# Mixed mLSTM and MLP block on one core: head stacks placed behind the first four MLP tiles, gate weights in one 128-column tile, decay exponents in half precision

## The chip, the cores and the metric

The kernel runs on one core of one Trainium2 chip. The metric is the device time of one launch in microseconds (us). A core has a matrix engine, TensorE (PE; its weight loads are shown apart as PEld), a vector engine (DVE), a scalar engine (ACT), GpSimd (POOL), and the DMA queues, here all issued by SyncE (SP). The engines run on their own and meet at semaphores.

## The reference, cut to what matters

The input is x of 8 sequences, 1024 tokens, 512 features, in float32. Everything reads one layer norm of x, and two branches are added to x:

```python
xn = _layernorm(x, axis=-1)
x = x + _L0_attn_ref(xn, Wq, Wk, Wv, Wog, Wig, big, Wfg, bfg, gamma, Wout) \
      + _L0_ffn_ref(xn, w_gate, w_up, w_down)
# attention: mLSTM, 8 heads, 32 query/key and 64 value features each
i_pre = soft_cap(x @ Wig.T + big)
f_pre = soft_cap(x @ Wfg.T + bfg)
f_log = log_sigmoid(f_t); m_new = maximum(f_log + m, i_t)
F = exp(f_log + m - m_new); I = exp(i_t - m_new)
C_new = F * C + (I * k_t) v_t;  n_new = F * n + I * k_t
h = einsum(q_t * scale, C_new) / (maximum(|q_t * scale . n_new|, exp(-m_new)) + EPS)
y = (sigmoid(x @ Wog.T) * headnorm(h) * gamma) @ Wout.T
# MLP, hidden size 2048
einsum(silu(gate) * up, w_down)
```

## The kernel before

The 8192 tokens are cut into 32 blocks of 256, and one hardware loop per engine runs 32 times over the blocks (`Fori(0, NB)`). The weights are loaded and split once, ahead of the loops. Each operand of a large product is kept as a high and a low half-precision part, and a product is three matmuls (`three`, L1006 to L1008: high by high, high by low, low by high). The recurrence is computed in chunks of 128 tokens.

What PE does in one block is written out by hand: the gate pre-activations (L1062 and L1064, eight matmuls), q and k (48 matmuls of 256 columns), v (24 matmuls of 512 columns), and then the 16 MLP tiles `ffn0` to `ffn15`, 24 matmuls of 256 columns each. The down projection of tile j, `down(j)`, six matmuls of 512 columns, stands behind tile j + 2. Pieces of the mLSTM stand behind given MLP tiles; a table of lists, `AFTER`, says which, and every engine walks through the same table. In it `stack3` is a piece for DVE alone, `stats` the layer norm statistics of the next block, `wT` and `wbc` the transpose and the spreading of the decay weights, `kT` the transpose of k, `es0` to `es3` the exponents and scores of two chunks and two groups of heads.

For tile j, ACT takes the tanh of the gate half (L640), DVE makes two products with the PSUM bank (L879, L882; the second one releases the bank), ACT writes the high part (L644), POOL the low part (L530), and `down(j)` waits for that. Three PSUM banks, `work0` to `work2`, go round in the order of the list `USES`.

The head stacks: `stack(h)` is six DVE copies (L828 and L829 in turn) that put the high and low parts of q and k of head h of a group above one another in `qq` and `kk`, for the score matmul L1134. Three stacks stand ahead of `ffn0` in DVE's program, behind the two operations that make the low parts of q (L866) and k (L868), and the fourth behind `ffn0`. The score matmul of `es0` waits for all 24 copies. In `wT` DVE writes `we_r` (L896, L898), which PE's L1111 (`wbc`) waits for.

The decay exponents: for each pair of tokens of a chunk and each head the exponent is one matmul of 512 columns, L1128, of `pair_l` and `pair_r` into `e_bank`. They hold the terms as a rounded high part and a rest in the 32-bit format F32R. DVE writes `pair_l`, `uhl` and `a_hi` (L855 to L862); POOL writes `pair_r` from `uhl` and a diagonal (`pair`, L520), once before `ffn0`, and once behind `es1`.

The gate weights lie in one tile of 104 columns per slice of 128 features: high parts in columns 0 to 39, low parts from column 64 (`G_LOW`). L1062 uses all 104 columns with the high part of x, L1064 only the first 40 with the low part. ACT copies the rows from 64 on (L606) and DVE adds them to the first 40 (L833), which frees the bank.

Of the kernel before, what the change touches and what calls it, by code (L numbers as in the profile page):

```python
# [16 lines left out]
ALU = mybir.AluOpType  # L17
ACT = mybir.ActivationFunctionType
AX = mybir.AxisListType
F32 = mybir.dt.float32  # L20
F32R = mybir.dt.float32r
F16 = mybir.dt.float16
# [4 lines left out]
P = 128  # L27
D = 512
KC = D // P
BATCH, SEQ = 8, 1024  # L30
BLOCK = 256
# [3 lines left out]
NH, DQ, DV = 8, 32, 64  # L35
# [7 lines left out]
GR = 40  # L43
G_LOW = 64
# [34 lines left out]


AFTER = {j: [] for j in range(NJ)}
AFTER[0] = ["stack3"]
AFTER[2] = ["stats"]
AFTER[3] = ["wT"]
AFTER[4] = ["wbc", "kT", "es0"]
AFTER[5] = ["o0", "mean_var"]
AFTER[6] = ["es1", "pv0", "xn0"]
# [69 lines left out]
def mlstm_mlp_kernel(nc, x, w_dram, gate_bias, gamma, out):  # L157
    ctx = ExitStack()
    with ctx:
        def sb(name, shape, dt):  # L160
            return ctx.enter_context(nc.sbuf_tensor(name, shape, dt))
# [6 lines left out]


        wt = {n: sb(f"parts_{n}", [P, 2, c], F16) for n, c in WCOLS.items() if n != "gates"}  # L170
        w_gates = sb("parts_gates", [P, KC, G_LOW + GR], F16)
        w_qk = wt["qk"][:, :, :].rearrange("p h (k f) -> p h k f", k=KC)
        w_v = wt["v"][:, :, :].rearrange("p h (k f) -> p h k f", k=KC)
        w_o = wt["o"][:, :, :].rearrange("p h (k f) -> p h k f", k=KC)
# [29 lines left out]
        xt = sb("xt", [P, KC, 2, BLOCK], F16)  # L204
        we_r = sb("we_r", [GR, BLOCK], F32R)

        pair_r = sb("pair_r", [P, NH, P], F32R)
        pair_l = sb("pair_l", [P, BLOCK], F32R)

# [6 lines left out]
        at, off = {}, 0  # L218
# [31 lines left out]
        tg, lf, ip, bc, mm, wr = (at[n] for n in ("tg", "lf", "ip", "bc", "mm", "wr"))  # L250
        uu, aa = bc, ip
        we = at["tg"]
        uhl = at["uhl"].bitcast(F32R)
        a_hi = at["lf"].bitcast(F32R)
        state = at["state"].rearrange("p (g n) -> p g n", g=NG)
        upd = at["upd"]
        num = at["num"].rearrange("p (h e) -> p h e", h=NH)
# [102 lines left out]
        def bank(name):  # L360
            return work[bank_no(name)]
# [54 lines left out]
        def _(pool):  # L416
            g = nc.gpsimd
# [3 lines left out]
            def link(ins):  # L421
                own_k[0] += 1
                ins.then_inc(pool_set, 1)
                pool.wait_ge(pool_set, own_k[0])
# [20 lines left out]
                                     base=-first, pattern=[[-HG, NG], [-1, HG], [0, DQ]], channel_multiplier=1))  # L445
            link(g.memset(we_r[:, :].bitcast(F32), 0.0))
            link(g.memset(w_gates[:, :, GR:G_LOW], 0.0))
            link(g.memset(diag[:, :], 0.0))
            for first in (0, 32):
                link(g.affine_select(out=diag[:, :], in_=diag[:, :], compare_op=ALU.not_equal, fill=1.0, base=-first,  # L450
                                     pattern=[[-1, NH]], channel_multiplier=1))
            link(g.memset(pair_r[:, :, :].bitcast(F32), 0.0))
            for first in (64, 96):
                link(g.affine_select(out=pair_r[:, :, :], in_=pair_r[:, :, :].bitcast(F32),
                                     compare_op=ALU.not_equal, fill=1.0, base=-first,
                                     pattern=[[-1, NH], [0, P]], channel_multiplier=1))
            link(g.memset(pair_l[:, :].bitcast(F32), 0.0))
            link(g.memset(pair_l[0:NH, :].bitcast(F32), -1.0))
            link(g.memset(pair_l[32:32 + NH, :].bitcast(F32), -1.0))
            link(g.memset(own_head[:, :], 0.0))  # L460
            for h in range(HG):
                link(g.memset(own_head[h * DQ:(h + 1) * DQ, h * VW:(h + 1) * VW], 1.0))
# [25 lines left out]

            for name in ("qq", "kk", "wr", "tg", "state"):
                link(g.memset(at[name], 0.0))  # L490
            link(g.memset(uhl.bitcast(F32), 0.0))
            for r, names in enumerate(ROUNDS):

                a, b = pieces_before(names[0]), pieces_before(names[-1], PIECES[names[-1]])
# [20 lines left out]
            with pool.Fori(0, NB) as i:  # L515
                own = Count(pool_own, 8)

                def pair(c):

                    g.tensor_tensor(pair_r[0:GR, :, :],  # L520
                                    uhl[0:GR, c * P:(c + 1) * P].bitcast(F32).unsqueeze(1).broadcast_to((GR, NH, P)),
                                    diag[0:GR, :].unsqueeze(2).broadcast_to((GR, NH, P)),
                                    ALU.mult).then_inc(pair_ready, 1)

                pool.wait_ge(parts_ready, i + 1)
                pair(0)
                for j in range(NJ):

                    pool.wait_ge(h_hi, i * NJ + j + 1)  # L529
                    g.tensor_tensor(hh[:, j % HB, 1, :], tt[:, j % 2, :], hh[:, j % HB, 0, :],  # L530
                                    ALU.subtract).then_inc(h_ready, 1)
                    for step in AFTER[j]:
                        if step.startswith("es"):

                            k = int(step[-1])
                            pool.wait_ge(exp_done, START + i * 4 + k + 1)
                            own.step(g.tensor_tensor(begun[0:1, 15:16], half_pow[0:1, 0:1], half_pow[0:1, 1:2],  # L537
                                                     ALU.add))
                            rows = pm[:, k % 2, :].rearrange("p (h t) -> p h t", h=HG)
                            g.affine_select(out=rows, in_=rows, compare_op=ALU.is_ge, fill=0.0, base=0,  # L540
                                            pattern=[[0, HG], [1, P]], channel_multiplier=-1).then_inc(masked, 1)
                        if step == "es1":

                            pool.wait_ge(e_full, i * 4 + 2)
                            pair(1)
                        if step.startswith("scale"):

                            pool.wait_ge(var_ready, i * NCH + int(step[-1]) + 1)
                            g.tensor_tensor(rd, var, half_pow[:, :], ALU.pow).then_inc(rd_ready, 1)  # L549
                        if step == "mean_var":  # L550

                            pool.wait_ge(stats_ready, NCH * (i + 2))
                            norm_factors(i, own)
                own.close()
# [130 lines left out]
        def _(dve):  # L685
            d = nc.vector

            k = [0]
# [131 lines left out]
            with dve.Fori(0, NB) as i:  # L820
                own = Count(dve_own, DVE_OWN)

                def stack(h):

                    rows = slice(h * DQ, (h + 1) * DQ)
                    for n, (q_part, k_part) in enumerate(((0, 0), (1, 0), (0, 1))):
                        to_ = slice((h + n) % HG * DQ, ((h + n) % HG + 1) * DQ)
                        d.tensor_copy(qq[to_, :, h, :], qp[rows, q_part, :, :]).then_inc(stacks_ready, 1)  # L828
                        d.tensor_copy(kk[to_, :, h, :], kp[rows, k_part, :, :]).then_inc(stacks_ready, 1)  # L829
# [17 lines left out]
                for c in range(NCH):  # L847
# [10 lines left out]
                own.settle(dve, i)  # L858
                own.step(d.tensor_scalar(m_carry, mm[0:NH, BLOCK - 1:BLOCK], keep[0:NH, bass.ds(i + 1, 1)], None,
                                         ALU.mult))  # L860
                own.step(d.tensor_tensor(uhl[32:32 + NH, :], uu[0:NH, :], uhl[0:NH, :].bitcast(F32), ALU.subtract))
                d.tensor_tensor(pair_l[96:96 + NH, :], aa[0:NH, :], a_hi[0:NH, :].bitcast(F32),  # L862
                                ALU.subtract).then_inc(parts_ready, 1)

                dve.wait_ge(qk_hi, 2 * (i + 1))
# [2 lines left out]
                own.step(d.scalar_tensor_tensor(out=kp[:, 1, :, :], in0=kf, scalar=unscale[:, NS + 2:NS + 3],  # L868
                                                in1=kp[:, 0, :, :], op0=ALU.mult, op1=ALU.subtract))
                own.settle(dve, i)  # L870
                stack(0)
                stack(1)
                stack(2)

                for j in range(NJ):

# [7 lines left out]
                                           op1=ALU.mult).then_inc(free_of(f"ffn{j}"), 1)  # L884
                    for step in AFTER[j]:
                        k_ = int(step[-1]) if step[-1].isdigit() else 0
                        if step == "stack3":
                            stack(3)
                        elif step == "stats":

                            dve.wait_ge(x_loaded, 16 * (i + 2))
# [32 lines left out]
                        elif step.startswith("pv"):  # L924

                            c, g = k_ // 2, k_ % 2
# [74 lines left out]
        def _(pe):  # L1001
            t = nc.tensor
# [32 lines left out]
            with pe.Fori(0, NB) as i:  # L1035
# [23 lines left out]
                pe.wait_ge(work_free[bank_no("xT1")], START + i * uses_of(bank_no("xT1")))  # L1059

                for k in range(KC):
                    t.matmul(bank("gates")[0:G_LOW + GR, 0:BLOCK], w_gates[:, k, :], xt[:, k, 0, :], start=(k == 0),  # L1062
                             stop=(k == KC - 1), skip_group_check=True)
                    mm_ = t.matmul(bank("gates")[0:GR, 0:BLOCK], w_gates[:, k, 0:GR], xt[:, k, 1, :], start=False,  # L1064
                                   stop=(k == KC - 1), skip_group_check=True)
                mm_.then_inc(work_full, 1)
                for name, f in (("q", 0), ("k", NH * DQ)):
                    wait_bank(pe, i, name)
                    for g in range(NG):
                        mm_ = by_feature(bank(name)[:, g * BLOCK:(g + 1) * BLOCK], w_qk, f + g * P, f + (g + 1) * P)  # L1070
# [5 lines left out]
                for j in range(NJ):  # L1076
# [5 lines left out]
                    for k in range(KC):  # L1082
                        if j in UNIT_IN:


                            c, g = UNIT_IN[j] // 2, UNIT_IN[j] % 2
                            mm_ = t.matmul(o_bank[:, k * VW:(k + 1) * VW], pm[:, UNIT_IN[j] % 2, k * P:(k + 1) * P],
                                           v[:, c, g * HG + k, :], start=False, stop=(k == HG - 1),
                                           skip_group_check=True)
# [7 lines left out]
                    for step in AFTER[j]:  # L1097
                        k = int(step[-1]) if step[-1].isdigit() else 0
# [8 lines left out]
                        elif step == "wbc":  # L1107

                            pe.wait_ge(we_split, i + 1)
                            for g in range(NG):  # L1110
                                mm_ = t.matmul(bank(step)[:, g * BLOCK:(g + 1) * BLOCK], spread[0:GR, g, :],  # L1111
                                               we_r[:, :], start=True, stop=True)
# [9 lines left out]
                        elif step.startswith("es"):  # L1122
                            c, g = k // 2, k % 2
# [5 lines left out]
                                     stop=True).then_inc(e_full, 1)  # L1129
# [9 lines left out]
                        elif step.startswith("pv"):  # L1139
                            c, g = k // 2, k % 2  # L1140
# [65 lines left out]
```

## Time and profile before

| | |
|---|---|
| time before, median of 3 runs | 3277.08 us (3275.98 to 3279.02) |
| the profiled execution: its time | 3273.61 us |
| the profiled execution: its span | 3271.9 us |
| mean granted TensorE clock | 0.992 of full speed |
| busy over the span: PE | 3101.0 us, 95% |
| PEld | 2229.5 us, 68% |
| DVE | 1876.5 us, 57% |
| ACT | 1116.8 us, 34% |
| POOL | 768.3 us, 23% |
| DMA | 51.08 MB, mean 16 GB/s |

The span goes from the first to the last instruction; the time of the execution lies 1.7 us above it. Matmuls are pipelined: the next one of a row starts before the record of the one before ends, so what a matmul costs is read from start to start. Line numbers are those of the kernel before.

### The profile page before, as it was taken

To read this page: it belongs to the slowest core of one execution; us is meant where nothing else is said; L and a number is where in the kernel's file an instruction comes from. 1 tells how busy PE (TensorE), PEld (TensorE's weight loads), DVE (VectorE), ACT (ScalarE), POOL (GpSimd) and SP (SyncE) were. 2 spreads that over 40 slices of the span, in tenths; PEclk is the share of its full clock that TensorE was granted. 3 is DMA by queue.
4 is the path that set the end of the run, shared out by engine and by line. 5 is a ranking of instruction groups with operands and counts; after the bars stand their busy time and mean duration, and the time that the engine had idled before them with its cause. 6 is when DMAs were issued, how large, how long until landed. Compare 5 with 4: busy or idle time off the path is not lost.

```text
span 3271.9 us, 61574 instructions
## 1 busy us (share of the span) xinstructions
PE 3101.0 (95%) x22408; PEld 2229.5 (68%) x22408; DVE 1876.5 (57%) x4361; ACT 1116.8 (34%) x2142; POOL 768.3 (23%) x1126
## 2 busy tenths in 40 slices
PE   1499999999999999999999999999999999999999
PEld 0377777677776677776677776677776677776676
DVE  5565555565555565555665555655555655555654
ACT  3433333333333333333333333333333333333332
POOL 4322222222222222222222222222222222222122
PEclk9799999999999999999999999999999999999999
DMA  5000000000000000000000000000000000000000
GB/s 213 7 14 7 6 13 13 13 13 6 6 13 13 13 13 6 6 13 13 13 13 6 6 13 13 13 13 6 6 13 13 13 13 6 6 13 13 13 13 6
DMA packets 20333, 51.08 MB, mean 16 GB/s; under 512 B 1506, under 2 KB 1634, under 8 KB 18274
## 3 DMA queue, kind: packets, MB, share of 16 engines
q1 hardware_dynamic: 20322, 50.95, 4.2%
q8 instruction: 6, 0.10, 0.0%
q14 instruction: 5, 0.04, 0.0%
HBM read 34.16 MB, written 16.78 MB: 16 GB/s over the span
## 4 chain that ended last, share of the span: by engine, by line
issue 74%; POOL 21%; PE 2%; ACT 1%; POOLq 1%; DVE 1%; DVEq 0%; ACTq 0%
POOL arena L530 9%; POOL pair_r L520 4%; POOL small L549 3%; POOL arena L540 2%; POOL begun L537 1%; POOL small L430 1%; PE work L1006 0%; PE work L1008 0%; PE work L1007 0%; POOLq L529 0%; POOL parts_u L481 0%; PE acc L1006 0%; DVE parts_d L740 0%; PE acc L1008 0%; PE acc L1007 0%
## 5 line engine op out<-in xcount | busy, mean ns | idle before, releaser
L530 POOL TENSOR_TENSOR arena<-arena 128x256 f16<-128x256 f32 x512 | 348.1, 680 | 1769.9 <-ACT arena L644 1769.9
L879 DVE SCALAR_TENSOR_TENSOR arena<-arena,work 128x256 f32<-128x256 f32 x512 | 215.8, 422 | 634.4 <-ACT arena L640 628.0
L1006 PE MATMUL work<-xt,parts_g 128*128 128x256 f16 x2048 | 558.4, 273 | 0.0
L1007 PE MATMUL work<-xt,parts_g 128*128 128x256 f16 x2048 | 558.3, 273 | 0.0
L1006 PE MATMUL work<-xt,parts_u 128*128 128x256 f16 x2048 | 558.2, 273 | 0.0
L1007 PE MATMUL work<-xt,parts_u 128*128 128x256 f16 x2048 | 558.2, 273 | 0.0
L1008 PE MATMUL work<-xt,parts_u 128*128 128x256 f16 x2048 | 558.2, 273 | 0.0
L1008 PE MATMUL work<-xt,parts_g 128*128 128x256 f16 x2048 | 558.2, 273 | 0.0
L1006 PE MATMUL acc<-parts_d,arena 128*128 128x512 f16 x1024 | 388.8, 380 | 56.6 <-POOL arena L530 56.6
L640 ACT ACTIVATE arena<-work,unscale 128x256 f32<-128x256 f32 x512 | 240.9, 470 | 583.6 <-PE work L1008 581.0
L644 ACT ACTIVATE arena<-arena 128x256 f16<-128x256 f32 x512 | 213.8, 418 | 645.5 <-DVE arena L882 645.5
L1007 PE MATMUL acc<-parts_d,arena 128*128 128x512 f16 x1024 | 388.6, 379 | 0.0
L1008 PE MATMUL acc<-parts_d,arena 128*128 128x512 f16 x1024 | 388.6, 379 | 0.0
L1006 PEld LDWEIGHTS work<-xt,parts_g 128*128 128x128 f16 x2048 | 228.1, 111 | 40.4 <-issue 0.3
L520 POOL TENSOR_TENSOR pair_r<-arena,diag 40x1024 fp32r<-40x1024 f32 x64 | 128.3, 2004 | 535.3 <-DVE pair_l L862 535.3
L1007 PEld LDWEIGHTS work<-xt,parts_g 128*128 128x128 f16 x2048 | 200.4, 98 | 40.7 <-issue 0.3
L882 DVE SCALAR_TENSOR_TENSOR arena<-arena,work 128x256 f32<-128x256 f32 x512 | 215.3, 420 | 17.5
L1008 PEld LDWEIGHTS work<-xt,parts_g 128*128 128x128 f16 x2048 | 200.4, 98 | 23.3
L1008 PEld LDWEIGHTS work<-xt,parts_u 128*128 128x128 f16 x2048 | 200.4, 98 | 23.2
L1006 PEld LDWEIGHTS work<-xt,parts_u 128*128 128x128 f16 x2048 | 200.4, 98 | 23.2
L1007 PEld LDWEIGHTS work<-xt,parts_u 128*128 128x128 f16 x2048 | 200.4, 98 | 23.2
L1006 PEld LDWEIGHTS acc<-parts_d,arena 128*128 128x128 f16 x1024 | 100.2, 98 | 134.5 <-issue 65.7
(214 smaller groups left out, 5503.9 us busy)
## 6 DMA issues: line engine op xcount, KB each, us to landing
arena<-x_dram SPq DMA_DIRECT2D x33, 512.0 KB, 3.3
out_dram<-arena SPq DMA_DIRECT2D x32, 512.0 KB, 2.8
parts_u<-w_g_dram SPq DMA_DIRECT2D x4, 1024.0 KB, 14.9
parts_d<-w_u_dram SPq DMA_DIRECT2D x4, 1024.0 KB, 22.8
arena<-w_d_dram SPq DMA_DIRECT2D x4, 1024.0 KB, 9.8
arena<-w_qk_dram SPq DMA_DIRECT2D x1, 1024.0 KB, 5.0
arena<-w_v_dram SPq DMA_DIRECT2D x1, 1024.0 KB, 7.0
arena<-w_o_dram SPq DMA_DIRECT2D x1, 1024.0 KB, 9.0
```

The costliest lines, as they stand in the source:

```text
L430: own.step(g.tensor_tensor(rstd, rstd, half_pow[:, 0:NCH], ALU.pow))
L520: g.tensor_tensor(pair_r[0:GR, :, :], uhl[0:GR, c * P:(c + 1) * P].bitcast(F32).unsqueeze(1).broadcast_to((GR, NH, P)), diag[0:GR, :].unsq ...
L530: g.tensor_tensor(hh[:, j % HB, 1, :], tt[:, j % 2, :], hh[:, j % HB, 0, :], ALU.subtract).then_inc(h_ready, 1)
L540: g.affine_select(out=rows, in_=rows, compare_op=ALU.is_ge, fill=0.0, base=0, pattern=[[0, HG], [1, P]], channel_multiplier=-1).then_inc(m ...
L549: g.tensor_tensor(rd, var, half_pow[:, :], ALU.pow).then_inc(rd_ready, 1)
L640: s.activation(tt[:, j % 2, :], bank(f"ffn{j}")[:, 0:BLOCK], ACT.Tanh, scale=unscale[:, sc["g"]:sc["g"] + 1]).then_inc(tanh_done, 1)
L644: s.activation(hh[:, j % HB, 0, :], tt[:, j % 2, :], ACT.Copy).then_inc(h_hi, 1)
L879: own.step(d.scalar_tensor_tensor(out=tt[:, j % 2, :], in0=tt[:, j % 2, :], scalar=1.0, in1=b[:, 0:BLOCK], op0=ALU.add, op1=ALU.mult))
L882: d.scalar_tensor_tensor(out=tt[:, j % 2, :], in0=tt[:, j % 2, :], scalar=HS, in1=b[:, BLOCK:2 * BLOCK], op0=ALU.mult, op1=ALU.mult).then_ ...
L1006: t.matmul(dst, w[0], a[0], start=first, stop=False, skip_group_check=True)
L1007: t.matmul(dst, w[0], a[1], start=False, stop=False, skip_group_check=True)
L1008: return t.matmul(dst, w[1], a[0], start=False, stop=last, skip_group_check=True)
```

## The change

Four edits. The three stacks ahead of `ffn0` and the one behind it become one behind each of `ffn0` to `ffn3`. The gate weights get 24 further columns of zeros and are used with all 128 columns for both parts of x. `pair_l`, `pair_r`, `uhl` and `a_hi` become half precision. The memsets ahead of the loops follow.

```diff
-AFTER[0] = ["stack3"]
-AFTER[2] = ["stats"]
-AFTER[3] = ["wT"]
+AFTER[0] = ["stack0"]
+AFTER[1] = ["stack1"]
+AFTER[2] = ["stack2", "stats"]
+AFTER[3] = ["stack3", "wT"]
...
-        w_gates = sb("parts_gates", [P, KC, G_LOW + GR], F16)
+        w_gates = sb("parts_gates", [P, KC, P], F16)
...
-        pair_r = sb("pair_r", [P, NH, P], F32R)
-        pair_l = sb("pair_l", [P, BLOCK], F32R)
+        pair_r = sb("pair_r", [P, NH, P], F16)
+        pair_l = sb("pair_l", [P, BLOCK], F16)
...
-        uhl = at["uhl"].bitcast(F32R)
-        a_hi = at["lf"].bitcast(F32R)
+        uhl = at["uhl"].bitcast(F16)[:, 0:BLOCK]
+        a_hi = at["lf"].bitcast(F16)[:, 0:BLOCK]
...
+            link(g.memset(w_gates[:, :, G_LOW + GR:P], 0.0))
...
                     g.tensor_tensor(pair_r[0:GR, :, :],
-                                    uhl[0:GR, c * P:(c + 1) * P].bitcast(F32).unsqueeze(1).broadcast_to((GR, NH, P)),
+                                    uhl[0:GR, c * P:(c + 1) * P].unsqueeze(1).broadcast_to((GR, NH, P)),
                                     diag[0:GR, :].unsqueeze(2).broadcast_to((GR, NH, P)),
...
                 own.settle(dve, i)
-                stack(0)
-                stack(1)
-                stack(2)
 
                 for j in range(NJ):
...
                     for step in AFTER[j]:
                         k_ = int(step[-1]) if step[-1].isdigit() else 0
-                        if step == "stack3":
-                            stack(3)
+                        if step.startswith("stack"):
+                            stack(k_)
...
                 for k in range(KC):
-                    t.matmul(bank("gates")[0:G_LOW + GR, 0:BLOCK], w_gates[:, k, :], xt[:, k, 0, :], start=(k == 0),
-                             stop=(k == KC - 1), skip_group_check=True)
-                    mm_ = t.matmul(bank("gates")[0:GR, 0:BLOCK], w_gates[:, k, 0:GR], xt[:, k, 1, :], start=False,
-                                   stop=(k == KC - 1), skip_group_check=True)
+                    for half in range(2):
+                        mm_ = t.matmul(bank("gates")[:, 0:BLOCK], w_gates[:, k, :], xt[:, k, half, :],
+                                       start=(k == 0 and half == 0), stop=(k == KC - 1 and half == 1))
                 mm_.then_inc(work_full, 1)
```

DVE's program before, from the low part of k (L868) to the products of `ffn1`; the copies between the two shown and L878 are 16 more, and four more stand behind the last pair shown:

```order
L868 SCALAR_TENSOR_TENSOR arena<-arena,unscale 128x512
L151 REGISTER_ALU
L828 COPY arena<-arena 32x2x256 [waits dve_own]
L829 COPY arena<-arena 32x2x256
...
L878 ISA
L879 SCALAR_TENSOR_TENSOR arena<-arena,work 128x256 [waits tanh_done]
L151 REGISTER_ALU
L882 SCALAR_TENSOR_TENSOR arena<-arena,work 128x256 [waits dve_own]
L828 COPY arena<-arena 32x2x256
L829 COPY arena<-arena 32x2x256
```

The same place in the changed kernel (its line numbers are 1 to 2 off: L870 is the low part of k, L878 and L881 the products, L830 and L831 the copies):

```order
L870 SCALAR_TENSOR_TENSOR arena<-arena,unscale 128x512
L152 REGISTER_ALU
L877 ISA [waits dve_own]
L878 SCALAR_TENSOR_TENSOR arena<-arena,work 128x256 [waits tanh_done]
L152 REGISTER_ALU
L881 SCALAR_TENSOR_TENSOR arena<-arena,work 128x256 [waits dve_own]
L830 COPY arena<-arena 32x2x256
L831 COPY arena<-arena 32x2x256
...
L877 REGISTER_ALU
L878 SCALAR_TENSOR_TENSOR arena<-arena,work 128x256 [waits tanh_done]
```

The 18 copies that stood ahead of the products of `ffn0` are gone from there; six copies stand between the products of one tile and those of the next.

DVE's program before, from the products of `ffn3` to those of `ffn4`, with the two operations of `wT` between them:

```order
L882 SCALAR_TENSOR_TENSOR arena<-arena,work 128x256 [waits dve_own]
L896 CAST we_r<-arena 8x256 [waits we_ready]
L151 REGISTER_ALU
L898 TENSOR_TENSOR we_r<-arena,we_r 8x256 [waits dve_own]
L878 REGISTER_ALU
L879 SCALAR_TENSOR_TENSOR arena<-arena,work 128x256 [waits tanh_done]
```

The same place in the changed kernel (L895 and L897 are the two of `wT`; two further pairs of copies stand at the dots):

```order
L881 SCALAR_TENSOR_TENSOR arena<-arena,work 128x256 [waits dve_own]
L830 COPY arena<-arena 32x2x256
L831 COPY arena<-arena 32x2x256
...
L895 CAST we_r<-arena 8x256 [waits we_ready]
L152 REGISTER_ALU
L897 TENSOR_TENSOR we_r<-arena,we_r 8x256 [waits dve_own]
```

Six copies now stand ahead of the two operations that PE's `wbc` waits for.

PE's first matmuls of a block before, two of the four pairs:

```order
L1062 MATMUL work<-xt,parts_gates 104x256
L1064 MATMUL work<-xt,parts_gates 40x256
L1062 MATMUL work<-xt,parts_gates 104x256
L1064 MATMUL work<-xt,parts_gates 40x256
L1062 MATMUL work<-xt,parts_gates 104x256
```

And in the changed kernel, up to the first of q:

```order
L1062 MATMUL work<-xt,parts_gates 128x256 x8
L1005 MATMUL work<-xt,parts_qk 128x256
L1006 MATMUL work<-xt,parts_qk 128x256
L1007 MATMUL work<-xt,parts_qk 128x256
L1005 MATMUL work<-xt,parts_qk 128x256
```

The number of matmuls is the same, eight; all of them now write 128 rows.

## Rows read from the trace of the kernel before

**Rows 1.** A stretch: us; busy (count) of PE, PEld, DVE, ACT, POOL; PEclk, DMA, GB/s.
```profile
2000.00:2100.00 100.00, 98.34 (x716) 70.94 (x714) 58.09 (x135) 34.53 (x69) 24.45 (x34) 1.00 0.03 10
```

**Rows 2.** Waits, whole span: who waited for whom, us, times, longest.
```profile
PE acc L1006 <- POOL arena L530: 56.6, 32, 3.4
...
PE work L1006 <- DVE arena L833: 45.1, 1, 45.1
```

**Rows 3.** Timeline of PE: start, duration, then the instruction; ffn0 to down(0).
```profile
2000.28 0.27 PE L1006 MATMUL work<-xt,parts_g 128*128 128x256 f16 x1
...
2008.03 0.27 PE L1008 MATMUL work<-xt,parts_u 128*128 128x256 f16 x1
2009.97 0.39 PE L1006 MATMUL acc<-parts_d,arena 128*128 128x512 f16 x1 [1.66 <-POOL arena L530]
```

**Rows 4.** Timeline of DVE, from the low part of k on, same block.
```profile
2000.69 2.38 DVE L868 SCALAR_TENSOR_TENSOR arena<-arena,unscale 128x512 f16<-128x512 f32 x1
...
2007.76 0.42 DVE L879 SCALAR_TENSOR_TENSOR arena<-arena,work 128x256 f32<-128x256 f32 x1
2008.22 0.42 DVE L882 SCALAR_TENSOR_TENSOR arena<-arena,work 128x256 f32<-128x256 f32 x1
2008.67 0.29 DVE L828 COPY arena<-arena 32x512 f16<-32x512 f16 x1
...
2009.20 0.79 DVE L828 COPY arena<-arena 32x512 f16<-32x512 f16 x1
...
2010.74 0.42 DVE L879 SCALAR_TENSOR_TENSOR arena<-arena,work 128x256 f32<-128x256 f32 x1
...
2013.26 1.28 DVE L747 BATCH_NORM_STATS2 small<-arena 128x6 f32<-128x512 f32 x2
...
2015.47 0.27 DVE L896 CAST we_r<-arena 8x256 fp32r<-8x256 f32 x1
2015.78 0.41 DVE L898 TENSOR_TENSOR we_r<-arena,we_r 8x256 fp32r<-8x256 f32 x1
```

**Rows 5.** Timeline of ACT, same block.
```profile
2003.52 0.47 ACT L640 ACTIVATE arena<-work,unscale 128x256 f32<-128x256 f32 x1
2008.67 0.42 ACT L644 ACTIVATE arena<-arena 128x256 f16<-128x256 f32 x1 [4.68 <-DVE arena L882]
```

**Rows 6.** Timeline of POOL, same block.
```profile
2000.07 2.46 POOL L520 TENSOR_TENSOR pair_r<-arena,diag 40x1024 fp32r<-40x1024 f32 x1 [16.94 <-DVE pair_l L862]
2009.17 0.67 POOL L530 TENSOR_TENSOR arena<-arena 128x256 f16<-128x256 f32 x1 [6.64 <-ACT arena L644]
```

**Rows 7.** Instructions of L828 and of L520: count, duration ns min/median/max.
```profile
L828 DVE COPY arena<-arena x384: 280/285/787, 132.8 to 3190.5; 32x512 f16<-32x512 f16 x192
...
L520 POOL TENSOR_TENSOR pair_r<-arena,diag x64: 1887/1890/2460, 129.8 to 3213.8; 40x1024 fp32r<-40x1024 f32 x64
```

**Rows 8.** Timeline of PE, the gate matmuls and the first of q.
```profile
1988.05 0.27 PE L1062 MATMUL work<-xt,parts_gates 128*104 128x256 f16 x1
1988.25 0.29 PE L1064 MATMUL work<-xt,parts_gates 128*40 128x256 f16 x1
...
1989.85 0.28 PE L1006 MATMUL work<-xt,parts_qk 128*128 128x256 f16 x1
```

**Rows 9.** Timeline of PE, the last of down(2) and wbc.
```profile
2019.02 0.38 PE L1008 MATMUL acc<-parts_d,arena 128*128 128x512 f16 x1
2019.33 0.50 PE L1111 MATMUL work<-we_r,spread 40*128 40x256 f32 x2
```

**Rows 10.** Timeline of PE, es1: the exponent and the score matmuls.
```profile
2030.71 0.38 PE L1007 MATMUL acc<-parts_d,arena 128*128 128x512 f16 x1
2030.93 0.38 PE L1008 MATMUL acc<-parts_d,arena 128*128 128x512 f16 x1
2030.96 0.58 PE L1128 MATMUL e_bank<-pair_r,pair_l 128*128 128x512 f32 x1
2031.38 0.40 PE L1134 MATMUL s_bank<-arena 128*128 128x128 f16 x4
```

More of the change, by code:

```diff
@@ L451, in _ @@
                                      pattern=[[-1, NH]], channel_multiplier=1))
-            link(g.memset(pair_r[:, :, :].bitcast(F32), 0.0))
+            link(g.memset(pair_r[:, :, :], 0.0))
             for first in (64, 96):
-                link(g.affine_select(out=pair_r[:, :, :], in_=pair_r[:, :, :].bitcast(F32),
+                link(g.affine_select(out=pair_r[:, :, :], in_=pair_r[:, :, :],
                                      compare_op=ALU.not_equal, fill=1.0, base=-first,
                                      pattern=[[-1, NH], [0, P]], channel_multiplier=1))
-            link(g.memset(pair_l[:, :].bitcast(F32), 0.0))
-            link(g.memset(pair_l[0:NH, :].bitcast(F32), -1.0))
-            link(g.memset(pair_l[32:32 + NH, :].bitcast(F32), -1.0))
+            link(g.memset(pair_l[:, :], 0.0))
+            link(g.memset(pair_l[0:NH, :], -1.0))
+            link(g.memset(pair_l[32:32 + NH, :], -1.0))
             link(g.memset(own_head[:, :], 0.0))
@@ L490, in _ @@
                 link(g.memset(at[name], 0.0))
-            link(g.memset(uhl.bitcast(F32), 0.0))
+            link(g.memset(uhl, 0.0))
             for r, names in enumerate(ROUNDS):
@@ L860, in _ @@
                                          ALU.mult))
-                own.step(d.tensor_tensor(uhl[32:32 + NH, :], uu[0:NH, :], uhl[0:NH, :].bitcast(F32), ALU.subtract))
-                d.tensor_tensor(pair_l[96:96 + NH, :], aa[0:NH, :], a_hi[0:NH, :].bitcast(F32),
+                own.step(d.tensor_tensor(uhl[32:32 + NH, :], uu[0:NH, :], uhl[0:NH, :], ALU.subtract))
+                d.tensor_tensor(pair_l[96:96 + NH, :], aa[0:NH, :], a_hi[0:NH, :],
                                 ALU.subtract).then_inc(parts_ready, 1)
```

## The prediction

> **What bounds the kernel now.** I read the busy times of a stretch first, then the waits, then the timeline of one block engine by engine. In a stretch of 100 us inside the loop PE is busy for 98.34 us at a granted clock of 1.00, and the next busiest engine, DVE, for 58.09 [rows 1]. So the loop is bound by PE, and only two things can shorten it: fewer or shorter steps on PE, and the idle time that is left there. The waits show one that comes back in each of the 32 blocks: the first matmul of a down projection waits for POOL's low part, 56.6 us in all [rows 2]. The other long one, 45.1 us for DVE's L833, happens once, in the first block, while DVE still works on the weights.
>
> The timeline of PE shows where the recurring one stands. From the first matmul of `ffn0` at 2000.28 to the last of `ffn2` at 2008.03 there are 71 steps in 7.75 us, 0.109 us each; the next matmul, the first of `down(0)`, should start at 2008.14 and starts at 2009.97 [rows 3]. That is 1.83 us; the row says 1.66, since a record's end lies 0.16 behind the point at which the next could have started. Over the span: 56.6 + 32 x 0.16 = 61.8 us.
>
> Why POOL is late: it follows ACT's L644, which follows DVE's products of `ffn0`. ACT had the tanh done at 2003.52 + 0.47 = 2003.99 [rows 5], and DVE had finished L868 at 2003.07, but its next product starts at 2007.76 [rows 4]: the 18 copies of three stacks stand between. From the product's start to `down(0)` it is then 2009.97 - 2007.76 = 2.21 us.
>
> **The stacks.** The work is the same, 24 copies; 18 of them move. Without them ahead, the product of `ffn0` starts when the tanh is done, 2003.99, and `down(0)` could start at 2006.20. PE reaches it at 2008.14, so the wait goes, with 1.94 us to spare. Gain: 61.8 us.
>
> What is late next? Now six copies stand behind the products of each of the first four tiles. The rows before show one such turn, `ffn0` to `ffn1`: from product to product 2010.74 - 2007.76 = 2.98 us, 0.91 for the two products and 2.07 for the six copies [rows 4]. One copy of the six takes 0.79 us instead of 0.28, and it starts 0.03 us after POOL's L530 at 2009.17, which ends at 2009.84 [rows 6]. Over the span L828's median is 0.285 and its maximum 0.787 [rows 7]. I take it that a copy which starts while POOL works on this tile is held until POOL is through: 0.5 us. Since POOL's L530 follows the products by a fixed chain, each of the four turns has its held copy.
>
> So DVE, in the times of the same block: `ffn0`'s product at 2003.99, four turns of 2.98 (11.92), the statistics behind the third (1.28), which brings L896 to 2017.19; L898 0.31 later, and 0.41 long [rows 4]: `we_r` is written at 2017.91. DVE never waits for a tanh on this stretch: `ffn3`'s product stands at 2014.21, and PE, six steps of 512 columns (twice 0.109 each) and 24 of 0.109 behind 2008.14, is through `ffn3` at 2012.07. PE for its part reached `wbc` at 2019.33 [rows 9] and now does 1.83 us earlier, at 2017.50. It waits 0.41, with a few hundredths for the way 0.45 us. That is a new stall of 32 x 0.45 = 14.4 us. Bounds: with no copy held DVE is 2.0 us earlier and the stall is nothing; with one more hold of 0.5 a block it is 0.95, or 30 us. `es0`'s scores, which need all stacks, stand behind `wbc` and the transposes, and the last copy ends ahead of L896, so they don't wait.
>
> The Trainium skill (GPSIMD Engine Reference, section 1, Specifications) says that GpSimd's SBUF interfaces are shared with VectorE and that they contend with DVE instructions in a 2-port perf mode or with two SBUF inputs. By that rule the copies are what it is about, and spreading them exposes all four groups instead of one; a plan that counts 0.28 us for each copy would give no new stall. The trace agrees for the one group that meets POOL now.
>
> **The gates.** From L1062's first start at 1988.05 to q's first at 1989.85 the eight matmuls take 1.80 us, 0.225 each, though they are 256 columns wide like q's [rows 8]. The 128-column matmuls of `ffn0` to `ffn2` step by 0.109 [rows 3]. All eight become of that form: 8 x 0.109 = 0.87 us, 0.93 less a block. In the first block PE waits for L833 anyway, so 31 blocks: 28.8 us. The bounds are nothing and 28.8; q's and `ffn0`'s rows are of the very form, so I take the full value. ACT's and DVE's chain behind the gates starts as much earlier as q does; it may be held some 0.4 us by the end of the block before, and `ffn0`'s product has 0.92 us of cover (2003.07 to 2003.99).
>
> The Trainium skill (TensorE: Matmul & The Clock Gate, "Weight-path perf modes") says that the fast weight load is on when the number of weights is 128 and the type is not FP32, which fits a gain here. But its section "LDWEIGHTS" prices a plain load at columns divided by 1.2 GHz, an estimate of 87 and 33 ns for 104 and 40 columns, both shorter than the 0.109 us of a step. If such loads were hidden, there would be nothing to gain; the rows with 0.225 a step say that they are not.
>
> **The exponents.** In `es1` the matmul L1128 seems to take 0.42 us to the next start, against 0.22 for one of half precision and the same 512 columns. But its start is recorded 0.03 us behind the start before, so it was still queued: from the last of `down` at 2030.93 to the scores at 2031.38 it is 0.45 for two matmuls, against 4 x 0.109 = 0.44 for twice 512 columns [rows 3, 10]. So 0.01 to 0.03 each, four a block, 128 in all: 3 us (0 to 6). POOL's L520 and DVE's small operations for `pair_l` change type; no row shows those forms. L520 now takes 1.89 to 2.46 us [rows 7], and DVE's L868 beside it 2.38. I take the same. As with the copies, L868 ends 0.54 us behind L520 [rows 4, 6], so a shorter L520 gains nothing (the tanh ends last), and one up to 3.4 us costs nothing.
>
> **The sum.** 61.8 + 28.8 + 3 - 14.4 = 79 us. The profiled execution took 3273.6, so 3194.4; the median of the runs shown is 3.5 above it, so **3198 us**.
>
> **The rivals.**
> - No new stall at `wbc`: the copies are not held each time, or POOL's operation falls between two of them. For it: the hold is seen in one group a block alone, and a few tenths decide. Then 3198 - 14 = 3184.
> - The gates gain nothing, since the step of 0.225 us has another reason than the width of the weights. Against it: q's and `ffn0`'s rows, which are of the form to come. Then 3198 + 29 = 3227. The Trainium skill's price of a plain load, named above, points this way.
> - The wait is moved and not removed: DVE does as much work ahead of `wbc` as before, and if its turns are 0.35 us longer than I read, PE waits the old 1.83 us at `wbc`. Then 3198 + 32 x 1.38 = 3242.
> - Slower than before: POOL's L520 on half precision takes much longer. It holds DVE's L868, and from 3.4 us on each microsecond delays `ffn0`'s product and, DVE being last all the way, is paid at `wbc`. It eats the 79 us (2.5 a block) at 5.9 us; at 7 us it is 3313. For it: no row shows the form; against it: the same 1024 elements on 40 partitions.
> - Nothing changes: if the wait moved on whole and the gates gained nothing, 3271 at most; I give it little.
>
> **How the numbers follow.** Forecast 0.62, with its own range of 3190 to 3208 (stall 0.2 to 0.75 us a block); no new stall 0.17; gates without gain 0.08; wait moved on 0.07; slower 0.03; no change 0.03. The range of 3180 to 3228 holds the first three. What a measurement of this kernel can tell from no change is 0.2%, 6.6 us. Faster by more 0.95, same 0.02, slower 0.03.
>
> **What the profile would show.** Right: no wait of PE in front of `down(0)`; a wait of about 0.45 us in front of the `wbc` matmul with DVE's L898 as releaser; the eight gate matmuls in 0.87 us; one copy of 0.79 in each of four groups, so a fourfold count. Wrong: a `wbc` wait of 0 or over 1 us, gate matmuls that still step by over 0.2 us, an L520 above 3.4 us, or a wait elsewhere that the timeline before doesn't have, such as at `es0`.

## The result and the profile after

The changed kernel takes **3189.36 us**, median of 4 runs (3187.99 to 3190.98), against 3276.62 us before in the same comparison: a ratio of 0.9733, 95% interval 0.9716 to 0.9749. That is 87 us less; 79 were forecast, and the time lies in the range of 3180 to 3228. The profiled execution took 3187.99 us with a span of 3186.3.

The busy times of the span and of the same 100 us of the loop as in [rows 1]:

```profile
PE 3062.1 (96%) x22408; PEld 2230.8 (70%) x22408; DVE 1917.7 (60%) x4361; ACT 1121.5 (35%) x2142; POOL 762.0 (24%) x1127
...
2000.00:2100.00 100.00, 99.74 (x736) 72.98 (x735) 61.01 (x141) 34.89 (x70) 22.27 (x34) 1.00 0.03 10
```

PE is now busy for 99.74 of 100 us, where it was 98.34. The waits of PE, those that come once a block and those that come once, against [rows 2]:

```profile
PE work L1005 <- DVE arena L835: 45.7, 1, 45.7
...
PE work L1109 <- DVE we_r L897: 9.0, 32, 1.0
```

The wait of `down(0)` for POOL is gone from the list, and one of 9.0 us in 32 blocks has come: `wbc` (L1109) for DVE's L897. The timeline of PE in one block, around the gates, around `wbc`, and at `es1`, against [rows 8 to 10]:

```profile
2032.69 1.04 PE L1062 MATMUL work<-xt,parts_gates 128*128 128x256 f16 x8
2033.56 0.27 PE L1005 MATMUL work<-xt,parts_qk 128*128 128x256 f16 x1
...
2060.88 0.38 PE L1007 MATMUL acc<-parts_d,arena 128*128 128x512 f16 x1
2061.52 0.47 PE L1109 MATMUL work<-we_r,spread 40*128 40x256 f32 x2 [0.26 <-DVE we_r L897]
...
2073.27 0.38 PE L1126 MATMUL e_bank<-pair_r,pair_l 128*128 128x512 f16 x1
2073.49 0.39 PE L1132 MATMUL s_bank<-arena 128*128 128x128 f16 x4
```

The eight gate matmuls take 0.87 us from start to start, where they took 1.80. From the last of `down(2)` to `wbc` it is 0.64 us; before, with nothing to wait for, it was 0.31. So PE waits 0.33. And the timeline of DVE from the low part of q on, against [rows 4]:

```profile
2043.98 2.48 DVE L868 SCALAR_TENSOR_TENSOR arena<-arena,unscale 128x512 f16<-128x512 f32 x1
2046.39 0.74 DVE L870 SCALAR_TENSOR_TENSOR arena<-arena,unscale 128x512 f16<-128x512 f32 x1
2047.73 0.42 DVE L878 SCALAR_TENSOR_TENSOR arena<-arena,work 128x256 f32<-128x256 f32 x1 [0.60 <-ACT arena L642]
2048.18 0.42 DVE L881 SCALAR_TENSOR_TENSOR arena<-arena,work 128x256 f32<-128x256 f32 x1
2048.52 0.28 DVE L830 COPY arena<-arena 32x512 f16<-32x512 f16 x1
...
2049.24 0.75 DVE L831 COPY arena<-arena 32x512 f16<-32x512 f16 x1
...
2050.54 0.42 DVE L878 SCALAR_TENSOR_TENSOR arena<-arena,work 128x256 f32<-128x256 f32 x1
...
2051.96 0.79 DVE L830 COPY arena<-arena 32x512 f16<-32x512 f16 x1
...
2056.48 1.29 DVE L749 BATCH_NORM_STATS2 small<-arena 128x6 f32<-128x512 f32 x2
2057.69 0.40 DVE L878 SCALAR_TENSOR_TENSOR arena<-arena,work 128x256 f32<-128x256 f32 x1
...
2060.96 0.41 DVE L897 TENSOR_TENSOR we_r<-arena,we_r 8x256 fp32r<-8x256 f32 x1
```

DVE waits 0.60 us for the tanh of `ffn0` and then for nothing until L897: the products, six copies with a long one among them, and the next products. In the whole trace 128 copies are long, four a block, where it was one a block.

Where the time went, from the starts of all matmuls, as means over 28 blocks of either trace (a block is 98.36 us before and 95.70 after):

```
wait at down(0)                        -1.88 us a block
gate matmuls and the step into q       -0.94
exponent and score matmuls, four times -0.13
wbc: its wait, less 0.03 in its matmuls +0.29
sum                                    -2.66
```

### The profile page after: what moved, and what is told of

Its sections match the earlier page's. It is cut to its first block, busy times and chain, and to the rows that moved or that the text cites. A ratio compares the mean times of both kernels' runs of the same rounds, so it can differ in the third digit from the quotient of the medians.

```text
span 3186.3 us, 61575 instructions
## 1 busy us (share of the span) xinstructions
PE 3062.1 (96%) x22408; PEld 2230.8 (70%) x22408; DVE 1917.7 (60%) x4361; ACT 1121.5 (35%) x2142; POOL 762.0 (24%) x1127
## 4 chain that ended last, share of the span: by engine, by line
PE 78%; DVE 11%; issue 6%; ACT 3%; POOL 1%; ACTq 0%; POOLq 0%; DVEq 0%
PE work L1007 17%; PE work L1005 16%; PE work L1006 16%; PE acc L1007 6%; PE acc L1006 6%; PE acc L1005 6%; DVE arena L831 3%; DVE arena L830 3%; PE o_bank L1085 3%; PE o_bank L1144 2%; PE work L1150 2%; DVE arena L878 2%; DVE arena L881 1%; ACT arena L636 1%; PE s_bank L1132 1%
## 5 line engine op out<-in xcount | busy, mean ns | idle before, releaser
L878 DVE SCALAR_TENSOR_TENSOR arena<-arena,work 128x256 f32<-128x256 f32 x512 | 214.9, 420 | 538.1 <-ACT arena L642 534.9
L522 POOL TENSOR_TENSOR pair_r<-arena,diag 40x1024 f16<-40x1024 f16 x64 | 122.5, 1914 | 514.5 <-DVE pair_l L864 514.5
L881 DVE SCALAR_TENSOR_TENSOR arena<-arena,work 128x256 f32<-128x256 f32 x512 | 215.4, 421 | 17.5
L920 DVE SCALAR_TENSOR_TENSOR arena<-s_bank,unscale,arena 128x512 f32<-128x512 f32 x128 | 95.9, 749 | 157.1 <-POOL arena L542 157.1
```

What stands on the lines that cost most here:

```text
L522: g.tensor_tensor(pair_r[0:GR, :, :], uhl[0:GR, c * P:(c + 1) * P].unsqueeze(1).broadcast_to((GR, NH, P)), diag[0:GR, :].unsqueeze(2).broa ...
L878: own.step(d.scalar_tensor_tensor(out=tt[:, j % 2, :], in0=tt[:, j % 2, :], scalar=1.0, in1=b[:, 0:BLOCK], op0=ALU.add, op1=ALU.mult))
L881: d.scalar_tensor_tensor(out=tt[:, j % 2, :], in0=tt[:, j % 2, :], scalar=HS, in1=b[:, BLOCK:2 * BLOCK], op0=ALU.mult, op1=ALU.mult).then_ ...
L920: d.scalar_tensor_tensor(out=pm[:, k_ % 2, :], in0=s_bank[:, :], scalar=unscale[:, NS + 3:NS + 4], in1=pm[:, k_ % 2, :], op0=ALU.mult, op1 ...
```

## The experiments

Unless it says otherwise, a time is the median of 5 runs. The runs of the kernel before beside them have medians of 3276.4 to 3277.0 us, so that differences to the changed kernel's 3189.4 can be read to about 1 us. Line numbers are those of each run's own kernel, a few off from one another.

**1. The stacks alone.** The kernel before with the table's new rows and the three stacks taken from their place ahead of `ffn0`.

```diff
-AFTER[0] = ["stack3"]
-AFTER[2] = ["stats"]
-AFTER[3] = ["wT"]
+AFTER[0] = ["stack0"]
+AFTER[1] = ["stack1"]
+AFTER[2] = ["stack2", "stats"]
+AFTER[3] = ["stack3", "wT"]
```

> The kernel before with the move of the stacks alone. My theory: the wait at down(0), 1.88 us a block by the difference of the two traces, goes, and about 0.3 us a block comes back at wbc behind DVE's L898; 32 blocks and about 1 us more in the first: 51 us less than before, 3225 to 3227. Rival (the parts depend on each other: without the shorter gates DVE keeps more lead and there is no wait at wbc): 61 us less, 3215. Rival (the stall comes back elsewhere): under 40 us less.

Measured: 3221.9 us, 55 us less than before; ratio 0.9834 (0.9821 to 0.9847). A block takes 96.77 us, 1.58 less: the wait at `down(0)` is gone, and `wbc` waits the same 0.3 us as in the changed kernel, so that wait isn't made by the shorter gates. Of the 55 us the two traces show 51, 1.58 in each of 31 blocks and 2.3 in the first, as I expected; the rest is not in the traces, which are of one execution each, and executions of the kernel before alone differ by 3 to 4 us.

**2. The gate weights alone.**

```diff
-        w_gates = sb("parts_gates", [P, KC, G_LOW + GR], F16)
+        w_gates = sb("parts_gates", [P, KC, P], F16)
...
+                    for half in range(2):
+                        mm_ = t.matmul(bank("gates")[:, 0:BLOCK], w_gates[:, k, :], xt[:, k, half, :],
...
```

> The kernel before with the 128-column gate weights alone. My theory: eight steps of 0.109 instead of 0.225, 0.93 us a block in 31 blocks, nothing else: 29 us less than before, 3247 to 3249. Rival (the engines behind the gates are bound by the end of the block before, and down(0)'s wait grows by what the gates give): less than 20 us, since DVE's L833 meets L996 and everything up to the product of ffn0 comes up to 0.4 us later against PE: 0.93 - 0.4 = 0.53 a block, 17 us less.

Measured: **3281.6 us** (11 runs, 3273.8 to 3290.3), 5 us more than before; ratio 1.0015 (1.0005 to 1.0025). Both expectations fell. The gate matmuls are 0.93 us shorter here too, and two things take that back. The waits:

```profile
PE acc L1007 <- POOL arena L531: 65.0, 32, 3.3
```

That was 56.6 [rows 2]. The rival was right so far: DVE's first operation for the gates, L834 (L833 before), no longer waits for ACT, but starts behind the last operation of the block before. First before, then here:

```profile
1989.04 0.75 DVE L996 SCALAR_TENSOR_TENSOR arena<-acc,unscale,arena 128x512 f32<-128x512 f32 x1
1990.37 0.42 DVE L833 TENSOR_TENSOR arena<-work,arena 40x256 f32<-40x256 f32 x1 [0.58 <-ACT arena L606]
```

```profile
317.12 0.75 DVE L997 SCALAR_TENSOR_TENSOR arena<-acc,unscale,arena 128x512 f32<-128x512 f32 x1
317.79 0.41 DVE L834 TENSOR_TENSOR arena<-work,arena 40x256 f32<-40x256 f32 x1
```

From there to the product of `ffn0` it is 17.45 us in either trace, and that operation comes 0.26 us later against q, so `down(0)`'s wait grows by 0.28 us a block. The other part I had not thought of: in 13 of 31 blocks the matmuls behind the wait are slow. The timeline of PE in one of them:

```profile
337.47 0.39 PE L1007 MATMUL acc<-parts_d,arena 128*128 128x512 f16 x1 [2.01 <-POOL arena L531]
337.69 0.38 PE L1008 MATMUL acc<-parts_d,arena 128*128 128x512 f16 x1
337.91 0.38 PE L1009 MATMUL acc<-parts_d,arena 128*128 128x512 f16 x1
338.12 0.52 PE L1007 MATMUL acc<-parts_d,arena 128*128 128x512 f16 x1
338.44 0.63 PE L1008 MATMUL acc<-parts_d,arena 128*128 128x512 f16 x1
338.86 0.63 PE L1009 MATMUL acc<-parts_d,arena 128*128 128x512 f16 x1
```

From 338.44 on the steps are 0.43 us instead of 0.22: the granted clock fell from 2.4 to 1.2 GHz. Two stretches of 10 us around the same wait, the first in the block ahead of this one, show it in their PEclk, the third number from the end:

```profile
235.00:245.00 10.00, 7.98 (x62) 5.82 (x61) 8.59 (x26) 2.76 (x7) 2.01 (x3) 1.00 0.00 0
...
333.00:343.00 10.00, 7.99 (x53) 5.55 (x51) 7.81 (x23) 2.28 (x6) 2.01 (x3) 0.83 0.00 0
```

A block with the low clock takes 99.41 us, one without 97.73: 1.68 us. By means over 28 blocks: -0.94 for the gates, +0.28 for the wait, +0.79 for slower steps behind it. So the wait alone leaves 0.66 of the gain, and the low clock makes the loss. The profiled execution took 3275.96 us, less than the median; the slower ones show a lower mean clock, down to 0.981 for its 0.985.

**3. The exponents alone.** F32R to F16 for `pair_l`, `pair_r`, `uhl` and `a_hi` in the kernel before.

> The kernel before with the exponents in half precision alone. My theory: four matmuls a block that give back some 0.02 to 0.03 us each, with the score matmuls behind them 0.13 us a block: 4 us less, 3272 to 3273, which is within 0.2%. Rival (POOL's and DVE's operations on half precision also move the chain in front of the product of ffn0): another difference of over 10 us, of either sign.

Measured: 3272.95 us (11 runs), 4 us less; ratio 0.9989 (0.9980 to 0.9998). The theory of the matmuls held. By the starts of `es1`, 0.45 us from the last of `down` to the scores became 0.43, and the four score matmuls take 0.01 less. That is 0.13 us a block, but the wait at `down(0)` is 0.04 longer, so the traces show 0.09, some 3 us in all; a difference of 1 us to the median is within what executions differ by.

**4. The statistics later.** The changed kernel with one piece moved.

```diff
-AFTER[2] = ["stack2", "stats"]
+AFTER[2] = ["stack2"]
-AFTER[4] = ["wbc", "kT", "es0"]
+AFTER[4] = ["wbc", "kT", "es0", "stats"]
```

> The changed kernel with the statistics of the next block (1.28 us of DVE) moved from behind ffn2 to behind the pieces of ffn4. My theory: DVE is the last engine in front of wbc, so its wait of about 0.3 us a block goes: 9 us less than the changed kernel, 3180. Rival (PE waits at wbc for something else, or the statistics are late for the next block's norm): the time of the changed kernel, 3189, or more.

Measured: 3179.1 us, 10 us less than the changed kernel; ratio to before 0.9703 (0.9690 to 0.9717). `wbc` waits in the first block alone. DVE was last there.

**5. The statistics twice.** The changed kernel does more on DVE ahead of `wbc`.

```diff
-DVE_OWN = 58
+DVE_OWN = 60
...
                             stats(own.step)
+                            own.settle(dve, i)
+                            stats(own.step)
```

> The changed kernel with the statistics of the next block computed twice, which adds 1.3 to 1.4 us of DVE behind ffn2. Theory (DVE is last all the way to wbc): PE's wait there grows by the whole of it, 32 x 1.35 = 43 us: 3232. Rival (DVE has slack ahead of wbc, and the wait there is for something else): 3189.

Measured: 3272.3 us (8 runs, 3263.0 to 3277.3), 83 us more than the changed kernel, twice what I expected. The wait grows by 1.32 us a block, as in the theory (42 us). The other 1.25 us a block are again the low clock, here in 24 of 31 blocks. Two stretches of 20 us around `wbc`, a block with it and one without:

```profile
440.00:460.00 20.00, 18.42 (x124) 12.46 (x122) 10.46 (x26) 4.07 (x10) 4.19 (x10) 0.91 0.00 0
540.00:560.00 20.00, 18.43 (x137) 13.32 (x136) 10.20 (x26) 5.11 (x12) 6.72 (x14) 1.00 0.00 0
```

**6. All four stacks ahead of `ffn0`,** in the changed kernel otherwise.

```diff
-AFTER[0] = ["stack0"]
-AFTER[1] = ["stack1"]
-AFTER[2] = ["stack2", "stats"]
-AFTER[3] = ["stack3", "wT"]
+AFTER[2] = ["stats"]
+AFTER[3] = ["wT"]
...
+                for h in range(HG):
+                    stack(h)
```

> The changed kernel with all four stacks ahead of ffn0. DVE's product of ffn0 then waits for 24 copies, and PE waits at down(0) for about 2.18 us, as with the gates alone, and 1.57 more: 3.75 us a block; nothing is left at wbc. Theory with the clock left alone: 3189 + 32 x (3.75 - 0.3) = 3300. Theory that a wait of over 2 us lets the granted clock fall behind it, as in part of the blocks of the run with the gates alone, here in every block, for 1.7 us each: 3350 to 3360, and a mean clock of about 0.97.

Measured: 3343.6 us (4 runs), 154 us more than the changed kernel; ratio to before 1.0207 (1.0191 to 1.0223). `down(0)` waits 3.72 us more a block, `wbc` no longer waits, and 26 of 31 blocks have the low clock; with 1.33 us a block for it the parts make 4.76 x 32 = 152 us. The time lies between the two expectations and nearer to the second, since five blocks were spared.

**7. Gate weights of 104 columns for both parts,** in the changed kernel.

```diff
-        w_gates = sb("parts_gates", [P, KC, P], F16)
+        w_gates = sb("parts_gates", [P, KC, G_LOW + GR], F16)
...
-                        mm_ = t.matmul(bank("gates")[:, 0:BLOCK], w_gates[:, k, :], xt[:, k, half, :],
+                        mm_ = t.matmul(bank("gates")[0:G_LOW + GR, 0:BLOCK], w_gates[:, k, :], xt[:, k, half, :],
```

> The changed kernel with gate weights of 104 columns for both parts of x, eight matmuls of one form. Theory (the width costs: a load of fewer than 128 columns isn't hidden): the eight keep their old 0.22 us a step, 0.9 us more a block than with 128 columns, 28 us more than the changed kernel: 3217. Rival (the change of form from one matmul to the next costs, 104 columns and 40 in turn): eight equal ones step by 0.109, 3189.

Measured: 3189.6 us, the time of the changed kernel (3189.4). The theory of the width fell. The timeline of PE:

```profile
2035.96 1.04 PE L1061 MATMUL work<-xt,parts_gates 128*104 128x256 f16 x8
2036.83 0.27 PE L1004 MATMUL work<-xt,parts_qk 128*128 128x256 f16 x1
```

Eight steps in 0.87 us, the last of them from 104 columns into q's 128: that change costs nothing.

**8. 128 columns and 40 in turn,** in the changed kernel.

```diff
+                    t.matmul(bank("gates")[:, 0:BLOCK], w_gates[:, k, :], xt[:, k, 0, :], start=(k == 0),
+                    mm_ = t.matmul(bank("gates")[0:GR, 0:BLOCK], w_gates[:, k, 0:GR], xt[:, k, 1, :], start=False,
```

> The changed kernel with 128 columns for the high part of x and the first 40 alone for the low part. Theory (only loads of fewer than 128 columns are exposed): four of eight steps are long, 0.45 us more a block than the changed kernel, 14 us: 3203. Rival (the change of form costs): all eight are long, 28 us more: 3217.

Measured: 3217.4 us, 28 more than the changed kernel. Every step is long, those into 128 columns too:

```profile
2051.74 0.27 PE L1061 MATMUL work<-xt,parts_gates 128*128 128x256 f16 x1
2051.94 0.29 PE L1063 MATMUL work<-xt,parts_gates 128*40 128x256 f16 x1
2052.16 0.28 PE L1061 MATMUL work<-xt,parts_gates 128*128 128x256 f16 x1
```

**9. Four of 128 columns, then four of 40.** The same matmuls as in 8, grouped.

```diff
                 for k in range(KC):
                     t.matmul(bank("gates")[:, 0:BLOCK], w_gates[:, k, :], xt[:, k, 0, :], start=(k == 0),
+                for k in range(KC):
                     mm_ = t.matmul(bank("gates")[0:GR, 0:BLOCK], w_gates[:, k, 0:GR], xt[:, k, 1, :], start=False,
```

> The changed kernel with four matmuls of 128 columns for the high part of x first, and then four of 40 columns for the low part. Theory (each change from one width of weights to another costs 0.11 us, and nothing else does): two changes instead of eight, about 0.2 us a block more than the changed kernel: 3195. Rival (a matmul of 40 columns and the one behind it are slow whatever stands ahead): four or five long steps, 0.5 us a block: 3205.

Measured: 3197.0 us, 8 more than the changed kernel. The steps of one block, from start to start in ns, are 110, 109, 109, **203** into the first of 40 columns, then 121, 110, 109, and **205** into q. A matmul of 40 columns behind another of 40 costs what one of 128 does. What costs is the change between 40 columns and a wide load of 104 or 128, some 0.1 us each time; with alternating widths each of the eight steps has one, as before [rows 8]. Why 104 and 128 count as alike isn't shown.

**10. POOL behind the copies.** In the changed kernel POOL's low part of the first four tiles waits for the copies behind that tile.

```diff
                     pool.wait_ge(h_hi, i * NJ + j + 1)
+                    if j < HG:
+                        pool.wait_ge(stacks_ready, i * 6 * HG + 6 * (j + 1))
```

> The changed kernel, in which POOL's low part of ffn0 to ffn3 waits until the six copies behind that tile are done, so that no copy meets it. Theory (a copy that starts while POOL works on the tile is held): a turn of DVE takes 2.48 us instead of 2.98, DVE is 2 us earlier at L897, and the wait at wbc goes, while the low parts come 1.1 us later, which down(0) has cover for: 9 to 10 us less than the changed kernel, 3180. Rival (the long copies have another cause, such as their place behind the product): the turns stay, 3189.

Measured: **3178.0 us**, 11 less than the changed kernel; ratio to before 0.9701 (0.9688 to 0.9714). No copy is long any more, and `wbc` doesn't wait. Durations of the copies, min/median/max in ns, in the changed kernel and then here:

```profile
L830 DVE COPY arena<-arena x384: 274/286/798, 134.5 to 3112.8; 32x512 f16<-32x512 f16 x192
```

```profile
L832 DVE COPY arena<-arena x384: 273/285/291, 134.2 to 3100.9; 32x512 f16<-32x512 f16 x192
```

**11. A longer operation for `pair_r`.** In the changed kernel POOL writes a second tile in the same operation, which nothing reads.

```diff
+        pair_both = sb("pair_both", [P, 2, NH, P], F16)
+        pair_r = pair_both[:, 0, :, :]
```

> The changed kernel, in which POOL's operation for pair_r of the first chunk writes two tiles instead of one, the second unused, so that it takes about 3.8 us in one piece. Theory (as in the rival that ends slower: DVE's L868 or L870 is held to its end, and then the product of ffn0 comes late): L870 ends some 0.85 us behind the tanh of ffn0, and DVE being last all the way, wbc's wait grows by it: 32 x 0.85 = 27 us, 3216; with a low clock behind part of the waits up to 3230. Rival (POOL's operation doesn't hold DVE beyond what it does now): 3189.

Measured: 3230.4 us (4 runs), 41 more than the changed kernel. The operation takes 3.60 us instead of 1.89, and `wbc`'s wait grows by 1.24 us a block. DVE's operation beside it, L868 in the changed kernel, has a median of 4.20 us instead of 2.49: it is held to the end of POOL's. The mechanism was right, my size of 0.85 too small. POOL is 1.71 longer, and only 0.46 of that is absorbed ahead of the product of `ffn0`: DVE's idle time there falls from 0.60 to 0.14 us, and the product starts 1.24 later. The first turn takes 2.81 us in both. I had counted the second of the two low parts (L870 in the changed kernel) as the held one and the first as done; in most blocks the first is held, and the second still follows. No block has the low clock.

The two fastest, 10 and 4, have no wait left at `wbc` and take the same 95.41 us a block.

## Why the prediction was right

**The wait at `down(0)`** went as forecast: 1.88 us a block, and in the first block 3.6 and 1.4 in the slow steps behind it, 63 us in all for the 61.8 of the sum. Runs 1 and 6 show that the copies ahead of the product made it.

**The gates** gave the forecast 0.93 us a block, but not for the reason that I read off q's rows, the width of the weights itself; in this point the right number is luck. The price lies in the change between 40 columns and the wide load ahead or behind (runs 7 to 9). I had the rival that 0.225 us a step had another reason than the width; it has, and the gain comes all the same, since the change removes the alternation too. The Trainium skill's rule that the fast weight load wants 128 weights (TensorE: Matmul & The Clock Gate, "Weight-path perf modes") doesn't explain the gain: by it the 104 columns of run 7 get no fast load, and they step by 0.109 us all the same.

**The sum treated the terms as independent, and they are not.** Run 2 is the proof: the gates alone cost 5 us, since DVE comes 0.28 us a block later against PE and the longer wait brings the low clock. Beside the moved copies they give their full 28 us (run 8 against the changed kernel): there DVE waits 0.87 us for the tanh of `ffn0`, and the shorter gates only cut that to 0.60. The prediction named such a cover of 0.92, and the 0.4 us by which the block before would hold DVE; it didn't say that the gain hangs on it.

**The copies** are held by POOL, four times a block: shown by run 10, which takes the meeting away. This agrees with the Trainium skill's rule on the shared SBUF interfaces (GPSIMD Engine Reference, section 1); which mode the copies run in, no trace shows.

**The new wait at `wbc`** is the term that was mis-sized: 0.29 us a block for 0.45, 10 us in all for 14.4. DVE's way from the product of `ffn0` to L897's end was put at 13.92 us and is 13.64. The first turn takes 2.81 us for 2.98, since its copies start 0.34 behind L881 and not 0.45 and its long copy is shorter, and the statistics cost 1.21 from start to start, where I took the row's 1.28. The other way, `wbc` starts 0.15 us behind L897's end, where I allowed 0.04, and part of the first error is hidden by that. That DVE is last all the way was right (runs 4 and 5).

**The exponents** gave 4 us for 3, as run 3's median does; its trace shows 3.

The terms as measured make 63.3 + 29.1 + 4.0 - 10.2 = 86 us; the spans differ by 85.6. Of the 7 us by which my sum was short, the wait at `wbc` is 4. (My 56.6 + 32 x 0.16 is 61.7 and not 61.8, which changes nothing.)

**The rival that ends slower** had the right mechanism and a wrong threshold: not 3.4 us for POOL's operation, but by run 11 some 1.89 + 0.46 = 2.35, an estimate. On half precision the operation takes what it took (1.884 to 2.454 us), so it didn't come to that.

**What stays open** is why the clock fell in some blocks and not in others. From the matmul ahead of the wait to the one behind it, and blocks with the low clock:

```
before          down(0)   1.92 to 2.03 us    0 of 31
exponents alone down(0)   2.02               0 of 31
gates alone     down(0)   2.18 to 2.30      13 of 31
four ahead      down(0)   3.76 to 3.87      26 of 31
longer pair     wbc       1.79 to 1.90       0 of 31
stats twice     wbc       1.95 to 1.97      24 of 31
```

The length of the wait alone doesn't order them: 2.03 us at `down(0)` was never followed by it, 1.95 at `wbc` mostly. Within the run of the gates alone the low clock goes with the longer waits: the seven blocks with 2.18 to 2.19 us kept the full clock, and 13 of the 24 with 2.28 to 2.30 lost it. What stands around `wbc`, small float32 matmuls and transposes, may matter; no run takes that apart.

## What to carry to other kernels

When one engine bounds a loop, ask of each saving on it which other engine's chain starts at that point: what is taken from the bound engine alone may come back in part as its next wait, as 0.28 of the gates' 0.93 us a block did until DVE had slack, and a longer wait can cost clock as well. Work that is moved out of a wait is paid again at the next place where its engine is last; add up its durations to that place, with what they meet there, and then move the piece that nobody waits for (the statistics). Keep small matmuls with narrow weights (40 columns here) together, or give them the width of their neighbours.

## What was not expected of the hardware

- From a matmul whose weights have 128 or 104 columns to one with 40, or back, a step of 256 columns takes 0.20 to 0.24 us; between equal ones, of 128, 104 or 40, and from 104 to 128, it takes 0.11 to 0.12.
- A stall of PE can cost more than its length. After 2.2 us or, at another place, 1.6 us of waiting, the granted clock fell to 1.2 GHz behind it in a part of the blocks, for up to another 1.7 us each. This doubled the price of run 5, and it turned run 2 from a gain into a loss.
